# Two-pass vision block on one core: the 3x3 convolution regrouped, one value region, new hand orders

## What is computed

```python
# first block: shifted-window attention, cosine similarity
qn = q / max(norm(q), 1e-12); kn = k / max(norm(k), 1e-12)
attn = softmax(qn @ kn * exp(logit_scale) + position_bias + mask)
x = x + (attn @ v) @ proj_w + proj_b
# feed-forward with sign weights; activations are scaled by the
# absolute maximum of a group of 3 images (15 of the 16 images take part)
x = x + bitlinear(gelu(bitlinear(LN(x), W1)), W2)
# second block: attention whose keys and values are sampled at learned places
q = LN(x) @ w_q + b_q
t = conv3x3(q, w_off0, groups=6) + b_off0
t = gelu(LN(t));  offset = tanh(t @ w_offp) * 8
xs = bilinear_sample(LN(x), offset + grid)
k, v = xs @ w_k + b_k, xs @ w_v + b_v
x = x + softmax(q @ k / sqrt(8)) @ v @ w_o + b_o     # 12 heads, 256 x 256
# four experts, the best two of each token, hidden width 384
x = x + sum(gate[e] * expert_e(LN(x)))
```

## Time and profile before

| | us |
|---|---|
| median of three runs (959.75 to 962.46) | 961.82 |
| the profiled execution, its own time | 962.33 |
| span shown by its profile | 960.5 |
| last values of the first pass to the first transpose of the second | 309.15 to 323.14 |
| first, fifth and last transpose `c_xt` of the second pass | 323.14, 437.35, 815.9 |

### The profile page before, as it was taken

The page is one execution under the profiler, slowest core; times in us unless marked ns, Lnnn a source line. Parts: engine busy times, 40 slices in busy tenths (PEclk is TensorE's granted clock), DMA queues, the critical chain, the costliest instruction groups (busy, mean ns, idle before and its releaser), DMA issues.

```text
span 960.5 us, 24087 instructions
## 1 busy us (share of the span) xinstructions
PE 825.3 (86%) x9578; PEld 617.8 (64%) x9578; DVE 499.0 (52%) x1288; ACT 566.8 (59%) x1037; POOL 406.3 (42%) x981
## 2 busy tenths in 40 slices
PE   2588588888988657789999999999999999989877
PEld 1366467676766544556776777777668667766655
DVE  5434554656654125556556556555755645664311
ACT  1345566666665212447756766866775676686642
POOL 3666766666653112334244234334424423431121
PEclk9989799999999676789999999999999999999997
DMA  3320000000000053245325414513522531550000
GB/s 71 73 80 2 2 3 2 7 10 7 11 6 8 1 143 107 65 118 145 91 55 145 122 47 127 144 45 102 144 88 59 144 113 50 130 148 14 5 5 5
DMA packets 42194, 63.45 MB, mean 66 GB/s; under 512 B 18897, under 2 KB 35458, under 8 KB 42082
## 3 DMA queue, kind: packets, MB, share of 16 engines
q1 hardware_dynamic: 41218, 61.61, 24.6%
q10 hardware_dynamic: 864, 0.30, 0.1%
HBM read 43.00 MB, written 17.31 MB: 63 GB/s over the span
## 4 chain that ended last, share of the span: by engine, by line
PE 71%; ACT 8%; issue 7%; DVE 6%; POOL 5%; DMA 1%; SPq 0%; ACTq 0%; DVEq 0%; POOLq 0%
PE ps L1042 65%; PE ps L1047 5%; ACT c_prob L999 2%; DVE a_xn L605 1%; POOL arstd L467 1%; DVE nm L792 1%; ACT c_stackt L987 1%; ACT a_prob L909 1%; ACT a_hb L937 1%; ACT a_stackt L987 1%; PE ps L1349 1%; PE ps L1200 1%; DVE astats L597 1%; ACT a_stackt L904 0%; DVE xa L708 0%
## 5 line engine op out<-in xcount | busy, mean ns | idle before, releaser
L792 DVE TENSOR_REDUCE nm<-ps 128x2 f32<-128x512 f32 x192 | 122.9, 683 | 61.1 <-PE ps L1042 59.7
L1031 ACT ACTIVATE a_prob<-ps 128x512 f32<-128x512 f32 (+1 forms) x128 | 62.8, 491 | 143.4 <-PE ps L1042 143.1
L1042 PE MATMUL ps<-c_xnt,we 128*128 128x256 f32 x384 | 115.8, 411 | 4.9 <-ACT a_prob L1031 4.8
L999 ACT ACTIVATE c_prob<-ps 128x512 f32<-128x512 f32 x192 | 104.8, 603 | 13.5 <-PE ps L1042 13.1
L1042 PEld LDWEIGHTS ps<-we,a_prob 128*128 128x128 f32 x768 | 94.3, 193 | 5.6 <-issue 3.2
L1042 PE MATMUL ps<-we,a_prob 128*128 128x96 f32 x768 | 96.5, 276 | 0.5 <-ACT a_prob L1031 0.5
L1042 PEld LDWEIGHTS ps<-c_xnt,we 128*128 128x128 f32 x384 | 65.0, 194 | 30.7 <-issue 14.9
L1042 PE MATMUL ps<-wconv,qpad 128*128 128x96 f32 x576 | 79.3, 298 | 2.4 <-ACT c_q L962 2.4
L1042 PEld LDWEIGHTS ps<-wconv,qpad 128*128 128x128 f32 x576 | 74.2, 210 | 9.1 <-issue 6.3
L784 DVE TENSOR_TENSOR wy<-wy,wx 128x768 f32<-128x768 f32 x64 | 58.6, 965 | 19.7 <-DMA wy<-row_scratch 19.6
L822 DVE SCALAR_TENSOR_TENSOR xc<-ps,gw,xc 128x96 f32<-128x96 f32 x128 | 34.6, 311 | 65.7 <-PE ps L1042 64.6
(11 more groups left out here) (235 smaller groups left out, 1816.2 us busy)
## 6 DMA issues: line engine op xcount, KB each, us to landing
wy<-row_scratch SPq DMA_DIRECT2D x32, 768.0 KB, 9.7
col_scratch<-hat SPq DMA_DIRECT2D x16, 768.0 KB, 4.7
wx<-col_scratch SPq DMA_DIRECT2D x16, 768.0 KB, 5.0
row_scratch<-hat SPq DMA_DIRECT2D x32, 96.0 KB, 2.2
xc<-xa SPq DMA_DIRECT2D x64, 24.0 KB, 5.7
out<-xc SPq DMA_DIRECT2D x16, 96.0 KB, 9.6
xa<-in_x SPq DMA_DIRECT2D x16, 48.0 KB, 2.0
xa<-in_x SPq DMA_DIRECT2D x32, 24.0 KB, 2.1
```

Of the source, the lines that this page charges most:

```text
L792: v.tensor_reduce(nm[i % 2][:, t, a, 2 * pq:2 * pq + 2], ps[:, 2 + a, :].rearrange("p (b n) -> p b n", n=TOK), AX.X, ALU.max, negate=True) ...
L999: a.activation(c_prob[:, u % 8], ps[:, 4 + u % 2, :], ACT.Exp, scale=float(HD) ** -0.5).then_inc(S("c_exp"), 1)
L1031: a.activation(c_hb[:, e % 2].rearrange("p m n -> p (m n)")[:, cols], ps[:, 6, 0:n_], ACT.Gelu).then_inc(S("c_h"), 1)
L1042: return m.matmul(o, l, r_, start=start, stop=stop)
```

## The change

- The convolution shifts the inputs: `shifted(b)` projects 32 channels from a zero-bordered `c_xntw` three times, shifted by a column, into three 32-row blocks (three sets of three matmuls), ACT copies these into `qpad`, nine matmuls of 32 columns accumulate the three row shifts, and since the result is transposed, ACT copies it (`convt`) and PE turns it back (`ct`). POOL makes the unpadded `c_xnt`.
- The three head groups accumulate into one region of 108 rows: values are stored with a stride `VAL`, `pv` accumulates, there is one `c_ot` copy, and two `sel` matmuls of 108 columns take the place of six in both passes. ACT writes the values in two copies in place of one.
- The third Newton step and the scale move from POOL to DVE; ACT copies q and k out of PSUM (`a_raw`), so banks 0 and 1 are released by ACT's `v`.
- First pass: `sel` and `proj` use bank 6, the feed-forward bank 7 alone, in two pieces.
- The gate's Exp becomes a power on POOL; ACT loads a table 42 times in the program in place of 74.
- The position-bias table is loaded and computed earlier, weights later; all order strings change, `C_FROM` goes from 13 to 24.

```diff
-    POOL="0311",  DVE="a13031322731637",  ACT="601012211111121",  PE="3223222202202021201",
+    POOL="6434",  DVE="b69da6465534663",  ACT="3347312123323222",  PE="13313132312232323222",
-    SP="d55",  POOL="aa568667",  DVE="396a979797777665495",
+    SP="2v2",  POOL="447543675",  DVE="6535354416235654544",
-C_FROM = 13
+C_FROM = 24
...
-                for _ in range(3):
+                for step in range(2):
...
+                own.link(g.tensor_tensor(e, euler[:], e, ALU.pow))
                 own.link(g.tensor_tensor(gt[:], other, e.to_broadcast(every), ALU.subtract))
...
+                own.link(v.scalar_tensor_tensor(third, scales, -0.5, scales, ALU.mult, ALU.mult))
+                own.link(v.tensor_tensor(third, third, ss[:, i % 2], ALU.mult))
+                own.link(v.scalar_tensor_tensor(scales, third, 1.5, scales, ALU.add, ALU.mult))
...
-                mm(ps[0:C, 0, 0:TOK], wq[:], c_xnt[:])
+                def shifted(b):
+                    for dx in range(3):
+                        ins = mm(ps[BLOCK * dx:BLOCK * dx + BLOCK, 0, TOK * (b % 2):TOK * (b % 2) + TOK], wq[:, BLOCK * b:BLOCK * b + BLOCK],
+                                 c_xntw[:, :, dx:dx + SIDE])
+                    return ins
+                shifted(0)
+                shifted(1).then_inc(S("c_qt"), 1)
...
-                for t in range(TILES):
-                    for k in range(9):
-                        r0 = 8 * t + k // 3
-                        ins = mm(tiles(0, C)[:, t, :], qpad[:, k % 3, r0:r0 + 8, :].rearrange("p r c -> p (r c)"), wconv[:, k, :], k == 0, k == 8)
+                for dy in range(3):
+                    for b in range(3):
+                        ins = mm(ps[BLOCK * b:BLOCK * b + BLOCK, 0, 0:TOK], wconv[:, dy, b, :], qpad[:, b, SIDE * dy:SIDE * dy + TOK], dy == 0, dy == 2)
...
-                    for s in range(3):
-                        at = (3 * t + s) * 4 * (HD + 1)
-                        ins = mm(ps[:, 1, at:at + 4 * (HD + 1)], c_ot[:, s, cols(t)], sel[:])
+                    ins = mm(tiles(1, HEADS * (HD + 1), TOK)[:, t, :], c_ot[:, cols(t)], sel[:])
```

More of the change, by code:

```diff
@@ L23 @@
 SLOT = 64
+VAL = 128 + HD + 1
+BLOCK = 32
+WIDTH = SIDE + 2
 SPLIT = 6 * HD
@@ L53 @@
     SP="b",
[L54 to L57, removed]
+    POOL="6434",
+    DVE="b69da6465534663",
+    ACT="3347312123323222",
+    PE="13313132312232323222",
 )
 C_ORDER = dict(
[L60 to L64, removed]
+    SP="2v2",
+    POOL="447543675",
+    DVE="6535354416235654544",
+    ACT="6566563767356533666663656535",
+    PE="67677674767746567666566637635767656353563566",
 )
-C_FROM = 13
+C_FROM = 24
 SETUP_TURN = 6
@@ L71 @@
 DVE_FIRST = 10
[L72 to L76, removed]
+DVE_SUMS = 12
+DVE_BIAS = 17
+DVE_WEIGHTS = 29
+DVE_PARTS = 39
+DVE_LAST = 48
+POOL_LAST = 14
 POOL_W1S = 1
-POOL_ZERO = 10
-POOL_ALL = 22
+POOL_ZERO = 11
+POOL_ALL = 23
 ACT_SCALE = 1
@@ L353, in _ @@
             load_x(0)
+            for t, name in cpb_loads:
+                sp.dma_start(t[:], A[name]).then_inc(cpb_in, 16)
             load_x(1)
@@ L437, in _ @@
             setup(g.memset(negone[:], -1.0))
+            setup(g.memset(euler[:], math.e))
             pool.wait_ge(setup_pool, POOL_ZERO)
@@ L453, in setup_last @@
                 setup(g.memset(qpad[:], 0.0))
+                setup(g.memset(c_xntw[:], 0.0))
                 for n in range(2):
@@ L526, in image_c @@
                 yield
+                need("xntw", i)
+                need("q", i - 1)
+                g.tensor_copy(c_xnt[:].rearrange("p (r c) -> p r c", c=SIDE), c_xntw[:, :, 1:1 + SIDE]).then_inc(S("c_xnt"), 1)
+                yield
+                need("cvar", i)
+                power(c_norm["conv"][i % 2], 1e-3).then_inc(S("c_crstd"), 1)
+                yield
                 need("qsb", i)
@@ L766, in image_c @@
                 yield
-                need("conv", i)
+                need("ct", i)
                 need("cn", i - 2)
-                stats(c_norm["conv"][i % 2], both(tiles(0, C))).then_inc(S("c_cvar"), 1)
+                stats(c_norm["conv"][i % 2], both(tiles(0, C, TOK))).then_inc(S("c_cvar"), 1)
                 yield
@@ L772, in image_c @@
                 need("tt", i - 1)
-                normed(c_norm["conv"][i % 2], both(tn), both(tiles(0, C))).then_inc(S("c_cn"), 1)
+                normed(c_norm["conv"][i % 2], both(tn), both(tiles(0, C, TOK))).then_inc(S("c_cn"), 1)
                 yield
@@ L980, in image_c @@
                 a.copy(c_k[:].rearrange("p t h c -> p t (h c)"), kv[:, :, 0:C]).then_inc(S("c_ksb"), 1)
-                a.copy(c_va[i % 3][:, :, :, 0:HD], kv[:, :, C:2 * C].rearrange("p t (h c) -> p t h c", c=HD)).then_inc(S("c_v"), 1)
+                for t in range(TILES):
+                    ins = a.copy(values_of(c_va[i % 3], slice(0, HD))[:, 3 * t:3 * t + 3],
+                                 kv[:, t, C:2 * C].rearrange("p (s q c) -> p s q c", s=3, c=HD))
+                ins.then_inc(S("c_v"), 1)
                 yield
@@ L1017, in image_c @@
                 a.copy(c_xnt3[0:C, :], ps[0:C, 6, TOK:2 * TOK]).then_inc(S("c_x3sb"), 1)
-                yield
-                need("gsub", i)
-                a.activation(sc[i % 2][:, 0], sc[i % 2][:, 0], ACT.Exp).then_inc(S("c_gexp"), 1)
                 yield
@@ L1414, in _constants @@
     c["flip"] = flip
-    sel = np.zeros((P, 4 * (HD + 1)), np.float32)
-    for j in range(4):
+    sel = np.zeros((P, HEADS * (HD + 1)), np.float32)
+    for h in range(HEADS):
         for k in range(HD + 1):
-            sel[32 * j + k, (HD + 1) * j + k] = 1
+            sel[32 * (h % 4) + (HD + 1) * (h // 4) + k, (HD + 1) * h + k] = 1
     c["sel"] = sel
@@ L1476, in _layout @@
         s = slice(GC * g, GC * g + GC)
-        wc[s, :, s] = w0[:, :, s].transpose(1, 0, 2)
+        b, at = GC * g // BLOCK, GC * g % BLOCK
+        for dx in range(3):
+            wc[BLOCK * dx + at:BLOCK * dx + at + GC, :, b, at:at + GC] = w0[dx::3, :, s].transpose(1, 0, 2)
         for a_ in range(2):
             wf[s, a_, g::DG] = np.broadcast_to(wp[:, a_:a_ + 1], (GC, SIDE))
-    wc[C, 4] = np.asarray(a["L1_conv_b_off0"])
+    wc[C, 1] = np.asarray(a["L1_conv_b_off0"]).reshape(3, BLOCK)
     L["wconv"], L["woffp"] = full(wc), full(wf)
```

262 lines of the change are left out of this document (148 added, 114 removed).

## The result

The changed kernel takes 979.16 us (median; 977.76 to 981.36) against 961.82: 1.0198 times as long, 95% interval 1.0155 to 1.0242. Predicted were 917, in a range of 885 to 945.

| stage, us | before | predicted | after | new order (e6, below) |
|---|---|---|---|---|
| start and first pass, to the start of its last values | 309.2 | 292.2 | 296.5 | 296.1 |
| to the first `c_xt` | 14.0 | 24.5 | 25.7 | 13.2 |
| first to fifth `c_xt` | 114.2 | 107.5 | 108.9 | 107.6 |
| eleven steady turns | 378.5 | 367.4 | 400.5 | 354.8 |
| last `c_xt` to the end | 144.7 | 123.5 | 147.9 | 143.0 |

The account below looks back on a forecast made before the run. PE's matmuls were taken to bound the steady second pass. From 962.3 us: start -10, first pass -7, handover +10.5, fill -6.7, steady turns -11, drain -21, sum -45, giving 917, range 885 to 945.

Parts of the forecast that it names:

- In this stage the time is PE's list of matmuls: Steady second pass: PE's matmuls set the 34.40 us turn, with 33.4 of PE work and 1.0 of waiting.
- The prices of the edits: Steady second pass, PE work a turn: 6.35 us removed, 3.8 added, net -2.5, leaving 30.9.
- Steady waits, 1.7 + 0.5 + 0.3: Steady turn, PE waits: 1.7 us at the turn of q, 0.5 for Exp pieces, 0.3 remaining of today's 1.0.
- Drain, 123.5: Last second-pass transpose to the end: a pipeline 0.7 turns shorter takes 123.5 us in place of 144.6, -21 us.
- Handover (+10.5): Between passes: two more feed-forward images (5.7 us) and half of 9.8 for a second quantisation precede the first transpose, +10.5 us.
- fill (-6.7): First to fifth second-pass transpose: feed-forward moved forward and shorter convolution, against some 4 us of longer chains, -6.7 us.
- Start (-10): Start and memsets: earlier bias table wins 3.5 us, memsets move behind a waiting chain; together -10 us (-13 to -3).
- first pass (-7): First pass: cheaper `sel` saves 14 us at most, exposed ACT copies and Newton steps would make it +4; middle, -7.
- 3 (column groups do not overlap): Six new matmul sets an image run one after another, 1.3 us each in place of 0.48; 977 us, chance 0.06.
- 2: DVE takes over: wait at the turn of q grows by 1, steady turn stays 34.4; 929 us, chance 0.2.
- 4: The orders do not fit: an engine's new order adds a 3 to 4 us wait a turn; 955 to 970, chance 0.09.
- three more visits of the column groups: Tiling-mode changes on PE: visits go from four to seven an image, 0.1 us each at most, about 5 in all.

Follow-up runs that it names:

- e6: All edits of the changed kernel with new second-pass strings: score rows spread singly, pipeline five images deep, second pass starting early; 921.55 us, 0.9618 times before.
- e2: The kernel before with one convolution tap of nine, leaving out 16 of 18 matmuls an image; 946.65 us against 960.9 (one run).
- e1: The changed kernel, all edits, with the second-pass order of the kernel before, new pieces put in; 970.08 us, 1.0092 times before.
- e4: The kernel before with only the 108-row value region, two `sel` matmuls for six, in the second pass, orders unchanged; 961.84 us, 1.001 times before.
- e5: All edits of the changed kernel with other second-pass strings: score rows spread singly, pipeline five images deep; 929.23 us, 0.9696 times before.
- e7: The kernel before without any edit, only its second-pass order changed to strings of the kind in e5 and e6; 963.81 us, 1.0063 times before.
- e9: The changed kernel with the gate's Exp back on ACT in place of POOL's power, other strings kept; 1004.52 us against 959.6 before (one run).
- e3: The changed kernel with DVE's row maxima reading half of the scores, 256 columns in place of 512; 956.18 us (one run).

## Why the prediction was wrong, point by point

- **"In this stage the time is PE's list of matmuls": the step that failed.** It took 97% busy for a bound. e2 and e1 show chains that come out as waits of PE as soon as work beside them goes, and e4 a chain that grew with what moved beside it. The prices of the edits held: PE work was put at 30.9 a turn, and in e6, where little waits, busy is about 31.1. In after a turn has 33.0 of busy and 3.0 of waits where the forecast had 30.9 and 2.5.
- **Steady waits, 1.7 + 0.5 + 0.3.** Mis-sized. I looked for one large wait, at the turn of q, and found its place; it is 1.04. But waits for `c_q`, single maxima, Gelu and `xc` add 1.9, and some 1.9 lie in rows that are busy for longer. I had counted "matmuls of other images between the pieces" as cover without laying each chain beside the rows that stand next to it. e5 and e6 show 0.7 to 0.8 of visible waits for the same edits. The wait at the turn of q has a further cause that I had not seen: POOL's two rows of parts, 0.94 + 0.81 in the earlier trace rows and again in after, stand beside DVE's products `wy`. In e7, with no row of DVE beside them, they take 0.29 + 0.31, and the 1.15 between is more than the wait. No run moved this pair alone. DVE before, then POOL in e7:

```profile
623.11 3.61 DVE L784 TENSOR_TENSOR wy<-wy,wx 128x768 f32<-128x768 f32 x4
...
624.79 0.29 POOL L539 CAST c_stack<-nm 128x24 bf16<-128x24 f32 x1 [1.13 <-DVE nm L792]
625.16 0.31 POOL L540 TENSOR_TENSOR c_stack<-nm,c_stack 128x24 bf16<-128x24 f32 x1
```

- **Drain, 123.5: wrong.** Its ends held: the first `sel` comes 4.9 us behind the last transpose, and 30.8 follow the last `sel`. The three turns between, priced at 85.9, took 112.1. That price came from the old pipeline, with the pipeline's length taken off (`sel` stood 0.80 of a turn behind that transpose before, not 0.85). The shorter pipeline does leave fewer matmuls behind the last transpose, but PE is busy with them for as long, at a lower clock (PE alone, stretch, length, busy, clock, DMA share, GB/s; before, then after):

```profile
815.82:960.50 144.68, 124.95 (x1016) 0.95 0.20 52
...
831.75:979.56 147.81, 124.53 (x907) 0.85 0.22 57
```

  Last transpose to the end took 140.5 to 152.5 in all eleven kernels, whether a pipeline of four images or of five. In after, `sel` does come early, but each turn then has more left to do, and at a lower clock. Windows from one `x3t` transpose to the next near the end of after, then of e6:

```profile
879.00:915.60 36.60, 32.46 (x250) 20.20 (x250) 15.79 (x36) 19.01 (x35) 12.61 (x27) 0.87 0.27 61
915.60:955.90 40.30, 32.86 (x191) 19.33 (x191) 11.06 (x29) 15.51 (x27) 7.06 (x20) 0.71 0.01 3
...
840.90:866.70 25.80, 22.51 (x192) 15.21 (x190) 10.87 (x29) 17.63 (x29) 7.12 (x20) 1.00 0.02 4
866.70:891.10 24.40, 17.84 (x132) 12.84 (x130) 4.75 (x19) 11.82 (x20) 6.56 (x18) 1.00 0.02 5
```

  191 records take 40.3 us at 0.71 in after, 192 take 25.8 at 1.00 in e6; the last such stretch has 191 records in after, 132 in e6. Why the clock fell there, and what sets the floor near 143, was not tried.
- **Handover (+10.5) and fill (-6.7): right** within 1.4 us each. The edits do not need the handover's cost: in e6, which begins the second pass earlier (and has other strings), it is 13.2.
- **Start (-10) and first pass (-7): 4.3 us short.** The bias table came 4.7 earlier, as the earlier trace rows allowed, and the 27.4 us turn with the memsets became one of 16.3 (from the values of one image to those of the next). But the first such turn rose from 17.7 to 27.05. PE in it, and DVE's row ahead of the first wait:

```profile
53.74 1.17 PE L1091 MATMUL ps<-perm_in,a_xn 128*96 128x128 f32 x4 [6.75 <-DVE a_xn L628]
58.12 1.17 PE L1091 MATMUL ps<-perm_out,a_on 128*96 128x128 f32 x4 [3.21 <-DVE a_on L638]
...
50.70 2.99 DVE L628 TENSOR_SCALAR a_xn<-xa,amv,arstd 128x96 f32<-128x96 f32 x2
```

  I had looked at POOL's queue. It is DVE's that is late: the nine rows of the feed-forward biases (43.08 to 50.7) stand ahead of this `a_xn`, which itself takes 2.99 us (see the last section), and its own memsets ahead of `a_on`.
- **Rivals.** 3 (column groups do not overlap) gave 977, close to the result, for a reason that the rows refute: a set takes 0.5. 2 named the place of one wait. 4 was the right case, priced too low, at 970 at most, since its band came from one wait and left the drain's gain standing.

Open: why the mean clock falls to 0.91 to 0.96 in some steady turns: 8 of 11 in e9 (3.9 us of visible waits in a turn), 2 in after (3.0), 5 in e2 (2.8), none in e1 (2.6) or e3 (1.9), but 2 in e7 (0.9) and 1 in e6 (0.7). It costs after some 3.9 us in the steady turns.

## What to carry to other kernels

When an engine is 97% busy in a kernel whose order was tuned, lay each chain between engines beside the rows that stand next to it before pricing a removal: the work may be there as cover; and look which rows of other engines the removal moves beside each other. Leaving the work out in the old kernel, one run, shows what an edit can be worth (1.0 of 4.0 us here). Edits and order are one change: the same edits lost 2% in one order and won 4% in another.

## What the runs showed of the hardware

A change of tiling mode (full array, 64 rows, 32 columns) is not free. In the kernel before, the six matmuls `we,a_prob` advance PE by 1.31 us behind a full-array row and by 1.41 behind a 50-row score (starts of the next rows):

```profile
599.41 1.47 PE L1042 MATMUL ps<-we,a_prob 128*128 128x96 f32 x12
600.72 0.84 PE L1042 MATMUL ps<-wkv,xst 128*128 128x192 f32 x4
...
604.38 1.58 PE L1042 MATMUL ps<-we,a_prob 128*128 128x96 f32 x12
605.79 0.38 PE L1338 MATMUL ps<-ident,c_on 128*96 128x128 f32 x2
```

About 0.1 us a change. A turn has 23 changes before, 28 after and 21 in e6, so order moves this cost too: 0.7 of the 1.9 us between after and e6, by that estimate. The Trainium skill ("TensorEngine Tiling (Array Packing)", "Key Properties") says that a change drains TensorE; the rows agree. The prediction counted three more visits of the column groups; the strings made two more, and three more of the 64-row scores.

Some rows of DVE and POOL took longer beside each other. The 2.99 us of `a_xn` above: the same two instructions take 0.57 at 63.80 of the same trace, and POOL was writing a memset of `c_stack` (2.74 us) through that stretch. In all eleven traces the normalisation beside these memsets took longer, 1.52 to 3.98 us; in the kernel before it is most of what DVE does in the 9.43 of the earlier trace rows once its own memsets are done:

```profile
107.66 3.84 DVE L605 TENSOR_SCALAR a_xn<-xa,amv,arstd 128x96 f32<-128x96 f32 x2
```

POOL's parts (0.60 alone, 1.75 beside `wy`) and the end of its key split (1.05 alone, in after and e6; 1.80 beside `th` and `hat`, in e4 and e1) are two more cases. That the one row slows the other was seen in each of these, not tested with nothing else changed.
